# Shifted attention: the last addition of every fourth unit moves from TensorE's transposes to VectorE

## What is computed

```python
K = jnp.stack([shift_time(k0, s) for s in (0, 4, 8, 12)], axis=2)
V = jnp.stack([shift_time(v0, s) for s in (0, 4, 8, 12)], axis=2)
att = jnp.einsum('bhtd,bhskd->bhstk', q / math.sqrt(16), K)
att = att + mask + alibi + jnp.log(pi + 1e-08)
att = jax.scipy.special.logsumexp(att, axis=2)   # over the 4 shifts
p = jax.nn.softmax(att, axis=-1)
ctx = jnp.einsum('bhtk,bhskd->bhtd', p, V)
```

## Time and profile before

| | us |
|---|---|
| median of three runs | 7602.68 (7565.14 to 7603.8) |
| the profiled execution, its own time | 7555.76 |
| span of the profile, first to last instruction | 7554.0 |
| around the span | 1.8 |
| shifted attention's 128 units in it | 486 to about 1012 |
| TensorE busy there, of 526.0 | 477.2 |
| GpSimd / VectorE / ScalarE busy there | 424.4 / 401.1 / 364.0 |

### The profile page before, as it was taken

The page is one execution under the profiler, slowest core; times in us unless marked ns, Lnnn a source line. Parts: engine busy times, 40 slices in busy tenths (PEclk is TensorE's granted clock), DMA queues, the critical chain, the costliest instruction groups (busy, mean ns, idle before and its releaser), DMA issues.

```text
span 7554.0 us, 47644 instructions
## 1 busy us (share of the span) xinstructions
PE 3587.5 (47%) x10858; PEld 1925.2 (25%) x10858; DVE 2987.1 (40%) x10577; ACT 2449.4 (32%) x6449; POOL 4565.1 (60%) x4472
## 2 busy tenths in 40 slices
PE   3569979623334444443444345433543444444334
PEld 1247754211112212221222122211221222122112
DVE  4667744443333333332333333433433333333301
ACT  1247733212333333332333333322332323332222
POOL 4238820046666666666666666766666666666764
PEclk8567866556666666666666666766666666666667
DMA  1000012211112221122122111212121122111221
GB/s 24 13 17 24 23 37 79 71 36 51 49 48 50 54 50 48 49 54 49 47 48 56 47 49 49 55 48 49 48 55 48 48 49 49 48 45 46 48 46 31
DMA packets 228682, 346.51 MB, mean 46 GB/s; under 512 B 111343, under 2 KB 150836, under 8 KB 228416
## 3 DMA queue, kind: packets, MB, share of 16 engines
q0 software_dynamic: 135168, 272.90, 15.0%
q1 hardware_dynamic: 93248, 70.74, 3.0%
HBM read 310.84 MB, written 32.52 MB: 45 GB/s over the span
## 4 chain that ended last, share of the span: by engine, by line
another core or an unknown queue 28%; DVE 24%; issue 22%; PE 5%; ACT 2%; DVEq 0%; ACTq 0%
DVE sq_is_cand L2027 3%; PE sq_ps_v L1764 3%; DVE sq_is_cand L2025 3%; DVE sq_row_f L2029 3%; DVE sq_kv L2075 2%; DVE sq_d_negmax L1934 2%; DVE sq_top_at L1996 1%; ACT sq_rows L1892 1%; DVE sq_c_negmax L2080 1%; DVE sq_sim_rest L1984 1%; DVE sq_top_at L1985 1%; DVE sq_tops L1992 1%; DVE sq_cand_rest L1984 1%; DVE sq_tops L1980 1%
## 5 line engine op out<-in xcount | busy, mean ns | idle before, releaser
L1676 POOL DMA_INDIRECT sq_rows<-in_L_ffn_table,sq_row x4096 | 4005.9, 978 | 2082.2 <-issue 1218.1
L1764 PE MATMUL sq_ps_v<-sq_rows,sq_ident 128*128 128x512 f32 x2048 | 1360.3, 825 | 953.3 <-remote 412.0
L1892 ACT ACTIVATE sq_rows<-sq_rows,sq_weight 128x128 f32<-128x128 f32 x4096 | 1250.7, 397 | 207.3 <-issue 200.2
L1764 PEld LDWEIGHTS sq_ps_v<-sq_rows,sq_ident 128*128 128x128 f32 x2048 | 532.5, 274 | 1648.6 <-issue 802.6
L1843 ACT ACTIVATE sq_prob<-sq_ps_c,sq_c_negmax 128x128 f32<-128x128 f32 (+3 forms) x256 | 135.1, 528 | 1726.6 <-remote 630.6
L1832 ACT ACTIVATE sq_exp_out<-sq_ps_d,sq_d_negmax 128x512 f32<-128x512 f32 x256 | 175.7, 686 | 1574.9 <-DVE sq_d_negmax L1934 771.8
L2075 DVE TENSOR_REDUCE sq_kv<-sq_ps_v 128x128 f32<-128x512 f32 x256 | 175.8, 687 | 1023.9 <-remote 739.7
L1722 PE MATMUL sq_ps_c<-sq_kT,sq_qT 64*128 64x512 f32 (+3 forms) x512 | 256.7, 588 | 437.8 <-issue 238.8
L1708 PE MATMUL sq_ps_t<-sq_ident,sq_kv 128*128 128x128 f32 x128 | 35.2, 429 | 814.5 <-DVE sq_kv L2075 554.6
L1700 PE MATMUL sq_ps_d<-sq_d_q,sq_d_k 64*128 64x512 f32 x512 | 348.5, 781 | 133.8 <-ACT sq_exp_out L1832 108.9
L1730 PE MATMUL sq_ps_t<-sq_ident,sq_prob 128*128 128x128 f32 x640 | 147.6, 340 | 553.2 <-ACT sq_kT L1838 317.2
(11 more groups left out here) (333 smaller groups left out, 5706.1 us busy)
## 6 DMA issues: line engine op xcount, KB each, us to landing
sq_rows<-in_L_ffn_table,sq_row POOLq DMA_INDIRECT x4096
qkvT<-exp_rows SPq DMA_DIRECT2D x32, 768.0 KB, 3.3
sq_d_q<-qkvT SPq DMA_DIRECT2D x8, 1024.0 KB
sq_d_k<-qkvT SPq DMA_DIRECT2D x32, 256.0 KB
sq_d_v<-qkvT SPq DMA_DIRECT2D x32, 256.0 KB
at_parts_dram<-at_parts SPq DMA_DIRECT2D x8, 384.0 KB, 2.3
at_qS<-at_parts_dram SPq DMA_DIRECT2D x48, 64.0 KB, 2.3
at_kS<-at_parts_dram SPq DMA_DIRECT2D x48, 64.0 KB, 2.3
```

What stands on the lines that cost most here:

```text
L1676: pool.indirect_dma_start(rows[u % GSLOTS][:, k, :], None, w2["table"], bass.IndirectOffsetOnAxis(row[tile % 3][:, h, k:k + 1], 0)).then_i ...
L1764: mm = pe.matmul(ps_v[:, :], ident[:, :], slot[:, 4 * k:4 * k + 4, :].rearrange("p k c -> p (k c)"), start=(k == 0), stop=(k == TOPK // 4 ...
L1892: ins = act.activation(slot[:, k, :], slot[:, k, :], ACT.Copy, scale=weight[tile % 3][:, h, k:k + 1])
```

## The change

- VectorE makes the second addition of the units with g % 4 = 3: a new function `last_addition(g)` adds the two halves of `psum_p` into `psum_all`. It waits for `added` of its unit and counts a new semaphore, `summed_dve`. It stands behind `inverse(g)`, in step g + 2, so one step ahead of TensorE's `transposes(g)`.
- All 128 units are transposed by four plain transposes. For the 32 units they wait for `summed_dve`, for the others for `summed`.
- `psum_all` has four buffers in place of three, taken by g % 4. GpSimd's instructions are the same as before, in number and order; ScalarE's too.

```diff
-def adds_both(g):
-    return g % 4 != 3
...
+def on_vector(g):
+    return g % 4 == 3
...
-        psum_all = [sb(f"psum_all{k}", [P, T]) for k in range(3)]
+        psum_all = [sb(f"psum_all{k}", [P, T]) for k in range(4)]
...
+                def last_addition(g):
+                    dve.wait_ge(S["added"], g + 1)
+                    dve.tensor_tensor(psum_all[g % 4][:, :], psum_p[g % 3][:, 0, :], psum_p[g % 3][:, 1, :], ALU.add).then_inc(S["summed_dve"], 1)
...
                             inverse(g - 2)
+                            if on_vector(g - 2):
+                                last_addition(g - 2)
...
-                    if adds_both(g):
-                        pe.wait_ge(S["summed"], both_so_far(g) + 1)
-                        for t in range(TT):
-                            mm = pe.transpose(ps_pT[:, t * P:(t + 1) * P], psum_all[both_so_far(g) % 3][:, t * P:(t + 1) * P], ident[:, :])
-                    else:
-                        pe.wait_ge(S["added"], g + 1)
-                        for t in range(TT):
-                            for j in range(NSH // 2):
-                                mm = pe.matmul(ps_pT[:, t * P:(t + 1) * P], psum_p[g % 3][:, j, t * P:(t + 1) * P], ident[:, :],
-                                               start=(j == 0), stop=(j == NSH // 2 - 1))
+                    pe.wait_ge(S["summed_dve" if on_vector(g) else "summed"], len(added_by(g)))
+                    for t in range(TT):
+                        mm = pe.transpose(ps_pT[:, t * P:(t + 1) * P], psum_all[g % 4][:, t * P:(t + 1) * P], ident[:, :])
```

More of the change, by code:

```diff
@@ L557, with added_by @@
 USE0 = bank_uses()
-def adds_both(g):
-    return g % 4 != 3
-def both_so_far(g):
-    return sum(adds_both(k) for k in range(g))
+def on_vector(g):
+    return g % 4 == 3
+def added_by(g):
+    return [k for k in range(g + 1) if on_vector(k) == on_vector(g)]
 def shifted_attention(nc, w, h_in, h_out):
@@ L641, in shifted_attention @@
         names = ("x_in x_used moments_ready std_ready xn_ready T_ps T_used high_ready middle_ready parts_made parts_stored stacks_in "
-                 "scores_ready scores_used max_ready probs_ready added summed pT_ps pT_ready ctx_ps context_part y_ready")
+                 "scores_ready scores_used max_ready probs_ready added summed summed_dve pT_ps pT_ready ctx_ps context_part y_ready")
         S = {n: sem(n) for n in names.split()}
@@ L921, in _ @@
                     pool.tensor_tensor(psum_p[g % 3][:, :, :], prob[g % 2][:, 0:2, :], prob[g % 2][:, 2:4, :], ALU.add).then_inc(S["added"], 1)
-                    if adds_both(g):
+                    if not on_vector(g):
                         pool.wait_ge(S["added"], g + 1)
-                        pool.tensor_tensor(psum_all[both_so_far(g) % 3][:, :], psum_p[g % 3][:, 0, :], psum_p[g % 3][:, 1, :], ALU.add).then_inc(S["summed"], 1)
+                        pool.tensor_tensor(psum_all[g % 4][:, :], psum_p[g % 3][:, 0, :], psum_p[g % 3][:, 1, :], ALU.add).then_inc(S["summed"], 1)
             @block.tensor
```

## The result

The changed kernel takes 7691.2 us (median of four runs, 7659.7 to 7701.8), the kernel before 7588.0 (four runs, 7565.1 to 7603.8). The ratio is 1.0141, with a 95% interval of 1.0117 to 1.0166: slower, by 89 to 126 us. The profiled execution of the changed kernel took 7659.7 us against 7555.8 before, +104.

What follows compares the result with a forecast made beforehand. TensorE, at 1.2 GHz throughout the stage, bounds every step. Batches 1 to 6 add 94 us, batch 7 9, batch 0 6, the tail -2.5: together +107 on a median of 7602.7, so 7710 us, range 7632 to 7750.

Steps and rivals of the forecast that it cites:

- The bursts raise the clock, without them it stays at 0.50: TensorE's clock in the stage: only the 32 removed bursts of eight f32 products raise it; without them 1.2 GHz throughout.
- rival 2: The stage's clock rises now and then, where scores, transposes and line 939 lie close: +50, 7650 us; chance 0.13.
- A unit takes 4.13 us, a batch 78.4 and 2.2: TensorE's instructions at 1.2 GHz, per unit and per batch, plus 2.2 us waiting for VectorE: 80.6 us a batch.
- Batch 0: The stage's first batch, at 0.50 up to 506.4 anyway, was to take 6 us more, with a wait.
- The sum for the stage: All terms together, batches 0 to 7 and the last burst gone from the tail: +107 us on the profiled execution.
- batches 3 to 6: Part of batches 1 to 6, forecast at 80.6 us each against 64.9 before: +15.7 each, +94 us for the six.
- the last: Batch 7, which prepares nothing: 66.7 us at 1.2 GHz against 57.4 before, +9 us.
- The wait for VectorE: TensorE waits for VectorE's new addition: 0.3 + 0.3 + 1.6 = 2.2 us a batch, bounds 0 and 7.4.
- VectorE stands still beside GpSimd: VectorE's new addition needs the ports shared with GpSimd: 0.69 us free, up to 2.53 us held up by GpSimd's instruction.
- Rival 1, the clock rises all the same: Plain scores and transposes suffice to raise the stage's clock: some 13 us won, 7590 us, no change; chance 0.12.

Runs made afterwards that it cites:

- e3: The changed kernel, but GpSimd makes the second addition of every unit and VectorE none; ratio 1.0084 to the kernel before.
- e4: The changed kernel, but for every fourth unit TensorE makes its four plain transposes four times over, 16 passes; ratio 1.0072 to the kernel before.
- e10: The changed kernel with the eight passes of the values made twice for every odd unit; one run, 7759.3 us.
- e1: The changed kernel, but every fourth unit also keeps the eight f32 products ahead of its four plain transposes; ratio 1.0084 to the kernel before.
- e7: The changed kernel with eight added f32 products on constant data behind the values of every fourth unit; ratio 1.0151 to the kernel before.
- e2: The kernel before, with VectorE's addition of every fourth unit also made, into a scratch tile nobody reads; ratio 1.0016.
- e11: The kernel before, but TensorE adds while transposing for three of four units, 96 bursts of eight f32 products in place of 32; ratio 0.9951.

## Why the prediction was right, and where it wasn't

- *The bursts raise the clock, without them it stays at 0.50.* Right for the mean (0.54) and for the first three batches; e3 and e4 show it from both sides. Wrong as "alone": the clock rose five times without a burst, in steps 6 and 7, behind four sets without values between them. Before, all seven such places ran at 1.00 already, so the trace of before could not show it. It is a small part of rival 2. Why two of the seven places of the changed kernel and all seven of e10 had no rise stays open.
- *A unit takes 4.13 us, a batch 78.4 and 2.2.* Batches without a rise took 80.3 us against 80.6, with 1.2 of waits in them and not 2.2; unrounded, the terms of the 78.4 add to 78.3. Batch 0 was forecast with +6 us; exponentials 0 to 16 went from 68.3 to 75.0 us, +6.6.
- *The sum for the stage* was +107 and the stage gave +84. The terms that were mis-sized are those of batches 3 to 6 (75.3 and not 80.6, 21 us in all) and of the last (63.6 and not 66.7), all by the five rises. That the whole came to +104 in the profiled execution and 1.0141 in the ratio is partly luck: some 20 us are in the last stage. The predicted 7710 also carried a median of before that a fourth run put 15 us lower.
- *The wait for VectorE.* 2.2 us a batch were forecast, 17.6 in all, and 20.3 measured. Its parts differ: 0.26 in most places (0.3 forecast); 0.63 in step 6 and not 1.6, for there the addition came late but wasn't held up (0.67 us long); and 2.2 to 2.8 five times in the stretches where the clock had risen, for which I had forecast nothing.
- *VectorE stands still beside GpSimd.* Right: 0.67 us free, up to 2.25 beside GpSimd's addition, as line 771. At the low clock the addition met at most the end of GpSimd's: 16 of the 32 took 0.88 us and ended some 0.54 us behind GpSimd's first addition, and 11 took 0.67 to 0.69.
- *Rival 1, the clock rises all the same.* It had "13 us won" at the clock of before. The runs at such a clock (e1, e4, e7) all lost, with 50 to 63 us of waits for VectorE. All three have other work added, so the price of exactly that case stays open. Its working put nothing for the next unit's maxima, which stand behind the addition; e2, where nobody waits for the addition, has a stage 21 us longer. That is more than the 13 us, so a gain is not what these runs suggest.

## What to carry to other kernels

Where TensorE's granted clock goes up and down within a stage, look in the trace for what it did before each rise, and ask of every edit that removes its work whether that work is what held the clock up. Passes saved can then be paid for by all passes left, and work given to TensorE can be faster than work taken from it (e11, where GpSimd was relieved as well). An addition of two SBUF tiles on VectorE that takes 0.67 us alone took up to 2.25 beside GpSimd's of 2.36, so don't put it in front of a waiting TensorE.

## What was unexpected of the hardware

- Sixteen plain transposes in a row raised the clock as well as sixteen passes of f32 products: 0.79 in e4, 0.78 before.
- The same instructions raised the clock in one batch or kernel and not in another: five of seven places of the changed kernel, none of seven in e10.
- TensorE was busy 99% of 730 us in e10 without one rise. The Trainium skill ("TensorE: Matmul & The Clock Gate", Part 1) has sustained matmul activity release the throttle. The trace of e10 doesn't bear that out as far as its busy time tells: it stayed at 0.50.
